# Two transformer layers on one core: 17 start-up weight loads move from SyncE's DMA queue to ScalarE's

## The chip, the cores and the metric

The kernel runs on one core of a Trainium2 chip. The metric is the device time of one execution in microseconds (us), lower is better. TensorE (PE), VectorE (DVE), ScalarE (ACT), GpSimd (POOL) and SyncE (SP) each run their own program in order and meet only through semaphores. Transfers between HBM and the on-chip memory are issued by an engine's program and carried out by 16 shared DMA engines; a semaphore rises when the data has landed.

## The reference

`x` is 64 sequences of 128 tokens with 256 features, `ctx` has the same shape. Two layers follow each other:

```
x = x + attn0(layernorm(x), ctx, ctx, mask)      # 16 heads of 16, biases on q, k, v, o
x = x + ffn0(layernorm(x))                       # 256 -> 1024 -> 256, weights quantised to -1, 0, 1
x = x + attn1(layernorm(x), ctx, ctx, lengths)   # no biases
x = ffn1(layernorm(x)) + x                       # chooses one of 8 experts by reconstruction loss
# quantisation in ffn0:
gamma = mean(abs(W)); Wq = clip(round(W / (gamma + eps)), -1, 1)
```

Quantising W1 and W2 (1 MB each) needs the whole matrix first, for gamma.

## The kernel before

The 64 sequences are worked through as 32 pairs. Everything that happens to one pair is cut into steps with a slot number from -14 to 77, and a new pair starts every 16 slots, so some five pairs are in flight. Each engine's program is a loop over the slots `t`; inside, `at(t, n)` picks the pair whose step `n` falls on slot `t`. The order in which an engine does its steps is thus written out by hand and fixed: a step that waits holds everything behind it on its engine.

SP issues every transfer, in one DMA queue. In program order at the start:

- `load(0)`: `xr`, `ctxT` and the two masks of pair 0 (L320 to L327).
- the seven loads of the list `EARLY` (L390): layer 0's `wk`, `wq`, `wv` and their biases. PE, DVE and ACT wait for all of them (semaphore `w_early`) before their loops.
- the two FFN matrices at L393 and L394, into `dif` (as `w1_ld`) and `hhl` (as `w2_ld`), tiles that later serve other ends; then the lengths (L395, L396) and `load(1)`.
- in the slot loop the round trips through HBM that bring queries and keys into another layout: `spill` (L334, `scr<-packed`) writes a pair's q or k out, `stack` (L354, `qs<-scr` or `ks<-scr`, four transfers) reads it back, and `maxima` (L370, `qs<-mrows`) puts row maxima under the queries.
- from slot -4 on, one transfer of the list `LATE` at the end of each slot (L432): 15 loads, among them `wo`, `wk`, `wq`, `wv` of layer 1, the base weights, the experts' `wd1s` and `wd2s`, and the biases `b1s`, `bd1s`, `bd2s`, which move element by element. Their first users wait for all 15 (`w_late`): PE at `output(0, 0)`, ACT, POOL and DVE later still.

DVE uses the FFN weights twice before the first scores: at slot -6 it waits for both matrices (`ffn_w_loaded`) and sums their absolute values (L1066, twice), turns the lengths into mask rows, and only then comes, in its program, to the query bias of pair 0 (`bias_q`, L817); POOL adds the sums over partitions (L579); at slot -2 DVE quantises (`quantise`, L769 to L778).

Pair 0's queries then go: DVE L817, ACT `high` (L613), DVE `low` (L832), SP `spill` (L334), SP `stack` (L354), and PE's scores (L1152), whose row maxima DVE takes (L859), with `exps` (L622) on ACT for the transposed scores (L1164).

```
if t == GAMMA_SLOT:
    dve.wait_ge(ffn_w_loaded, 32)
    for w, ld in enumerate((w1_ld, w2_ld)):
        nc.vector.tensor_reduce(gam[:, w:w + 1], ld, AX.X, ALU.add, ...)
```

Of the kernel before, what the change touches and what calls it, by code (L numbers as in the profile page):

```python
# [21 lines left out]
KD = D // P  # L22
# [3 lines left out]
KF = F // P  # L26
# [31 lines left out]
LATE_SLOT = -4  # L58
# [19 lines left out]
def ring(l, p):  # L78
    return (2 * p + 5 * l) % NR
# [16 lines left out]
def build(nc, x, lens, mask, mask_t, wq0, bq0, wk0, bk0, wv0, bv0, wo0, bo0, w1t, b1, w2t, b2,  # L96
          wq1, wk1, wv1, wo1, w_base, wd1, bd1, wd2, bd2, adapters, ctx_in, out):
    with ExitStack() as ctx:
# [6 lines left out]
        def sem(name):  # L105
            return ctx.enter_context(nc.semaphore(name))
# [84 lines left out]
        w1_ld = dif[:].rearrange("p e k t -> p (e k t)")  # L191
        w2_ld = hhl[:].rearrange("p a k t -> p (a k t)").bitcast(F32)
# [87 lines left out]
        w_early, w_late, ffn_w_loaded = sem("w_early"), sem("w_late"), sem("ffn_w_loaded")  # L280
# [12 lines left out]
        def rows(w):  # L293
            return w.rearrange("(k p) n -> p k n", p=P)
# [18 lines left out]
        @block.sync  # L313
        def _(sp):
            def load(p, ahead=False):
                if p < 2 and not ahead:
                    return
                if p >= NX:
                    sp.wait_ge(stored[p % 2], 16 * ((p - NX) // 2 + 1))
                sp.dma_start(xr[:, p % NX], xv[:, PB * p:PB * p + PB, :]).then_inc(x_loaded[p % 2], 16)  # L320
                k_ready[1].done(sp, p - NC)
                v_ready[1].done(sp, p - NC)
                sp.dma_start(ctxT[:, p % NC], ctx_in[p]).then_inc(ctx_loaded[p % 2], 16)
                mask_q.done(sp, p - 1)
                mask_k.done(sp, p - 1)
                sp.dma_start(mq_ld[:], mqv[:, PB * p:PB * p + PB, :]).then_inc(mask_loaded[p % 2], 16)
                sp.dma_start(mt_ld[:], mtv[:, PB * p:PB * p + PB, :]).then_inc(mask_loaded[p % 2], 16)  # L327

            def spill(l, j, p):
                ((k_high if j else q_high)[l]).done(sp, p)  # L330
                ((k_low if j else q_low)[l]).done(sp, p)
                if p >= 2:
                    sp.wait_ge(stacked[l][p % 2], STACK * (p // 2))
                sp.dma_start(scr[l][j][p % 2].rearrange("p m h d t -> (h d) p m t"), packed[l][j][:])\  # L334
                    .then_inc(scr_written[l][j], 16)

            def stack(l, j, p):
                dst = (ks if j else qs)[:, ring(l, p)]
                if l:
                    st_ready[0].done(sp, min(p + 1, NP - 1))  # L340
                    st_ready[1].done(sp, p - 3)
                else:
                    st_ready[1].done(sp, p - 4)
                    st_ready[0].done(sp, p - 3)
                sp.wait_ge(scr_written[l][j], 16 * (p + 1))
                if l and j and p == 0:
                    sp.wait_ge(len_steps, 4)
                    sp.dma_start(len_dram, len_rows[:]).then_inc(len_stored, 16)
                if j and p == 0:
                    sp.wait_ge(len_stored, 32 if l else 16)  # L350
                    sp.wait_ge(rows_set, 2)
                for n in range(4):
                    part = n % 2 if j else n // 2
                    sp.dma_start(dst[HD * n:HD * n + HD], scr[l][j][p % 2][part].rearrange("m h d t -> d (m h) t"))\  # L354
                        .then_inc(stacked[l][p % 2], 16)
                if j:
                    if l:
                        src = len_dram[PB * p:PB * p + PB].rearrange("(o b) t -> o (b t)", o=1)
                    else:
                        src = const_dram[0:1]  # L360
                    sp.dma_start(dst[MASK_ROW:MASK_ROW + 1], src.unsqueeze(1).to_broadcast([1, H, T]))\
                        .then_inc(stacked[l][p % 2], 16)

            def maxima(l, p, b):
                m_turned[l].done(sp, p, b)
                if l == 0 and p == 0 and b == 0:
                    sp.wait_ge(q_rows_set, 1)
                for n in range(4):
                    t0 = b * P + 32 * n
                    sp.dma_start(qs[MASK_ROW + 1:MASK_ROW + 3, ring(l, p), :, t0:t0 + 32],  # L370
                                 mrows[32 * n:32 * n + 32, l, b]).then_inc(m_landed[l][b], 16)

            def gather(p):
                up_ready.done(sp, p - 1)
                for b in range(PB):
                    expert_found.done(sp, p, b)
                    e = sp.value_load(lidx[0:1, b, 0:1], min_val=0, max_val=E - 1)
                    sp.dma_start(adapter[:, b], adapters[bass.ds(e, 1)].rearrange("a p n -> p (a n)"))\
                        .then_inc(gathered, 16)

            def store(p):
                y_ready.done(sp, p)
                if p >= 2:
                    sp.wait_ge(stored[p % 2], 16 * (p // 2))
                sp.dma_start(outv[:, PB * p:PB * p + PB, :], xr[:, p % NX]).then_inc(stored[p % 2], 16)

            load(0, True)
            with nc.allow_non_contiguous_dma(reason="biases, one or a few for each partition, once"):
                for dst, src in EARLY:
                    sp.dma_start(dst, src).then_inc(w_early, 16)  # L390
                sp.wait_ge(rows_set, 1)
                sp.dma_start(const_dram, const_rows[:]).then_inc(len_stored, 16)
                sp.dma_start(w1_ld.rearrange("p (k f) -> p k f", k=KD), rows(w1t)).then_inc(ffn_w_loaded, 16)  # L393
                sp.dma_start(w2_ld.rearrange("p (k d) -> p k d", k=KF), rows(w2t)).then_inc(ffn_w_loaded, 16)  # L394
                sp.dma_start(lens_c[:], lens.rearrange("(n a) -> n a", a=1)).then_inc(len_loaded, 16)  # L395
                sp.dma_start(lens_r[:], lens.rearrange("(a n) -> a n", a=1).to_broadcast([P, B])).then_inc(len_loaded, 16)  # L396
            load(1, True)
            for t in range(FIRST, END):
                for p in at(t, -14):
                    load(p)  # L400
                for p in at(t, 38):
                    spill(1, 0, p)
                for p in at(t, 6):
                    maxima(0, p, 0)
                for p in at(t, 38):
                    stack(1, 0, p)
                for p in at(t, 71):
                    gather(p)
                for p in at(t, -9):
                    spill(0, 1, p)  # L410
                for p in at(t, 7):
                    maxima(0, p, 1)
                for p in at(t, 24):
                    spill(1, 1, p)
                for p in at(t, -5):
                    stack(0, 1, p)
                for p in at(t, -4):
                    spill(0, 0, p)
                for p in at(t, 44):
                    maxima(1, p, 0)  # L420
                for p in at(t, -4):
                    stack(0, 0, p)
                for p in at(t, 76):
                    store(p)
                for p in at(t, 29):
                    stack(1, 1, p)
                for p in at(t, 45):
                    maxima(1, p, 1)
                if LATE_SLOT <= t < LATE_SLOT + len(LATE):
                    dst, src = LATE[t - LATE_SLOT]  # L430
                    with nc.allow_non_contiguous_dma(reason="biases, one or a few for each partition, once"):
                        sp.dma_start(dst, src).then_inc(w_late, 16)  # L432

            for k in range(2):
                sp.wait_ge(stored[k], 16 * (NP // 2))
# [147 lines left out]
        def _(act):  # L583
# [32 lines left out]
            def exps(l, p, j):  # L616
                st_ready[l].done(act, p, j)
                if l:
                    mix_ready[0].done(act, min(p + 2, NP - 1), j // 4)
                else:  # L620
                    mix_ready[1].done(act, p - 3, j // 4)
                nc.scalar.activation(pT[:, j], X[:], ACT.Exp, scale=SCALE).then_inc(exp_done[l].sem, 1)  # L622
# [51 lines left out]
                                         ACT.Relu, bias=adapter[R * b:R * b + R, b, AW - 1:AW]).then_inc(a_relu.sem, 1)  # L674

            act.wait_ge(w_early, 16 * len(EARLY))
            for t in range(FIRST, END):
                for p in at(t, 64):
                    squares(p, 0)
# [76 lines left out]
                    exps(1, p, 0)  # L756
                for p in at(t, 47):
                    exps(1, p, 1)

        @block.vector  # L760
        def _(dve):
# [682 lines left out]
```

## Time and profile before

| | |
|---|---|
| Runs | 1650.56, 1653.96, 1654.30 us; median 1653.96 |
| The profiled execution | 1655.75 us; its span, first to last instruction, 1654.0 us |
| TensorE busy | 1538.2 us, 93% of the span |
| VectorE, GpSimd, ScalarE busy | 1306.7, 1098.6, 892.6 us (79%, 66%, 54%) |
| DMA queues | one of transfers (SP's), 154.4 MB; two small ones for instructions |
| Mean granted TensorE clock | 0.965 |

Busy time is the sum of an engine's instruction times. The profile's page also shows the span in 40 slices of 41.35 us, a digit per slice in tenths. In the rows further down, "SPq" is a transfer being issued by SP (its duration is that of the issue, not of the data's way), "to landing" is the time from issue to the semaphore, and a name such as L1152 is a line of the kernel.

### The profile page before, as it was taken

How to read it: one execution, taken by the hardware profiler on the slowest of the kernel's cores; microseconds unless marked ns; L12 is line 12 of the kernel's file. 1: busy time of each engine (PE TensorE's matmuls, PEld its weight loads, DVE VectorE, ACT ScalarE, POOL GpSimd, SP SyncE). 2: the span in 40 equal slices, each digit the busy share in tenths (PEclk: the TensorE clock that was granted, in tenths of full speed). 3: DMA queues.
4: the chain of work that ended last, by engine and by line, in shares of the span. 5: the costliest groups of instructions: out<-in, count | busy, mean ns of one | idle time of the engine just before them, and what ended most of it. 6: DMA issues, size and time to landing. Idle time of an engine off the chain costs nothing.

```text
span 1654.0 us, 43794 instructions
## 1 busy us (share of the span) xinstructions
PE 1538.2 (93%) x15072; PEld 1270.5 (77%) x15072; DVE 1306.7 (79%) x5141; ACT 892.6 (54%) x2465; POOL 1098.6 (66%) x1197
## 2 busy tenths in 40 slices
PE   3588999999999999999999999999999999999865
PEld 2366888788888888888888888888888888887654
DVE  7456888888888888988888889888888898886552
ACT  0133555665555556655556566655565566555532
POOL 4476787766776777667767776667678766656300
PEclk7689999999999999999999999999999999999976
DMA  8447666456566665556566655565666555552320
GB/s 201 78 79 97 98 95 107 89 102 100 96 104 108 97 106 94 100 96 98 101 108 102 106 95 101 96 95 100 104 114 95 97 99 98 91 85 51 61 35 22
DMA packets 286479, 157.23 MB, mean 95 GB/s; under 512 B 39089, under 2 KB 281906, under 8 KB 286258
## 3 DMA queue, kind: packets, MB, share of 16 engines
q1 hardware_dynamic: 286258, 154.44, 55.3%
q8 instruction: 120, 1.97, 0.6%
q14 instruction: 101, 0.83, 0.2%
HBM read 111.36 MB, written 41.96 MB: 93 GB/s over the span
## 4 chain that ended last, share of the span: by engine, by line
PE 74%; DVE 9%; DMA 5%; issue 4%; POOL 3%; SPq 3%; ACT 1%; ACTq 0%; DVEq 0%; POOLq 0%
PE psD L1231 6%; PE psD L1189 6%; PE psD L1221 6%; PE psS L1152 6%; PE psV L1177 6%; PE psD L1210 6%; PE psD L1128 6%; PE psX L1164 6%; PE psD L1136 6%; PE psD L1202 5%; PE psD L1118 5%; DMA qs<-scr 4%; PE psD L1255 4%; PE psD L1101 3%; DVE dump L859 2%
## 5 line engine op out<-in xcount | busy, mean ns | idle before, releaser
L515 POOL TENSOR_TENSOR pT<-pT,keep 128x512 f32<-128x512 f32 x256 | 320.9, 1269 | 90.7 <-ACT pT L622 90.6
L622 ACT ACTIVATE pT<-psX 128x512 f32<-128x512 f32 x512 | 305.2, 596 | 110.7 <-PE psX L1164 105.3
L500 POOL TENSOR_SCALAR xn<-xr,mv,rstd 128x256 f32<-128x256 f32 x256 | 311.1, 1223 | 10.4
L474 POOL TENSOR_SCALAR veps<-mv 128x2 f32<-128x2 f32 x128 | 29.0, 226 | 360.1 <-DVE mv L794 357.8
L859 DVE CUSTOM_DVE_ANT_0 dump<-psS,bias 128x128 bf16<-128x128 f32 x1024 | 234.2, 283 | 23.3 <-PE psS L1152 21.7
L1152 PE MATMUL psS<-ks,qs 65*128 65x128 f16 x2048 | 202.0, 222 | 35.5 <-DMA qs<-scr 33.3
L925 DVE SCALAR_TENSOR_TENSOR dif<-psD,bd2s,xT 128x256 f32<-128x256 f32 x512 | 213.8, 466 | 13.0 <-PE psD L1231 12.9
L666 ACT ACTIVATE dif<-dif 128x256 f32<-128x256 f32 x512 | 207.6, 414 | 26.1 <-DVE dif L925 23.2
L1164 PE MATMUL psX<-qs,ks 67*128 67x128 f16 x2048 | 200.5, 220 | 14.2 <-ACT pT L622 10.1
L1152 PEld LDWEIGHTS psS<-ks,qs 65*128 65x128 f16 x2048 | 147.1, 99 | 85.3 <-issue 41.4
L851 DVE TENSOR_REDUCE mx<-psS 128x4 f32<-128x512 f32 x256 | 169.6, 671 | 23.2 <-PE psS L1152 23.0
L1164 PEld LDWEIGHTS psX<-qs,ks 67*128 67x128 f16 x2048 | 140.2, 98 | 49.1 <-ACT pT L622 17.3
L599 ACT ACTIVATE xT<-psD 128x512 f32<-128x512 f32 x96 | 57.2, 596 | 199.4 <-PE psD L1101 199.3
L520 POOL TENSOR_TENSOR hhl<-work,hhl 128x512 f16<-128x512 f32 x128 | 147.7, 1159 | 18.1 <-ACT hhl L652 15.4
L613 ACT ACTIVATE packed<-psD 128x512 f16<-128x512 f32 x96 | 57.3, 597 | 175.9 <-PE psD L1128 77.5
L1177 PE MATMUL psV<-pT,v 128*32 128x128 f32 x4096 | 139.9, 278 | 10.3 <-POOL pT L515 4.6
L1231 PE MATMUL psD<-hd,wd2s 64*128 64x256 f32 x1024 | 146.0, 404 | 2.6 <-DVE dif L925 2.6
L1118 PE MATMUL psD<-ctxT,wk 128*128 128x256 f32 x512 | 127.0, 392 | 11.2 <-DMA bvb<-in_bv 10.9
L1189 PE MATMUL psD<-wo,attT 128*128 128x256 f32 x512 | 130.4, 400 | 5.3 <-DVE attT L894 5.3
L1202 PE MATMUL psD<-xs,w1q 128*128 128x256 f16 x1024 | 132.9, 272 | 1.2 <-DVE xs L907 1.2
L646 ACT ACTIVATE work<-psD,b1s 128x256 f32<-128x256 f32 x256 | 107.8, 478 | 46.9 <-PE psD L1202 42.6
L1136 PE MATMUL psD<-wv,ctxT 128*128 128x256 f32 x512 | 131.3, 401 | 1.0 <-DVE packed L832 1.0
(96 smaller groups left out, 3125.8 us busy)
## 6 DMA issues: line engine op xcount, KB each, us to landing
scr<-packed SPq DMA_DIRECT2D x128, 256.0 KB, 2.9
ks<-scr SPq DMA_DIRECT2D x256, 128.0 KB, 5.4
qs<-scr SPq DMA_DIRECT2D x256, 128.0 KB, 4.3
adapter<-in_adapters SPq DMA_DIRECT2D x64, 192.5 KB, 2.5
xr<-in_x SPq DMA_DIRECT2D x32, 256.0 KB, 2.8
ctxT<-in_ctx SPq DMA_DIRECT2D x32, 256.0 KB, 2.7
qs<-mrows SPq DMA_DIRECT2D x512, 2.0 KB
out_y<-xr SPq DMA_DIRECT2D x32, 256.0 KB, 5.3
```

The source lines that it names most:

```text
L500: nc.gpsimd.tensor_scalar(xn[:, XN[s], b], xr[:, p % NX, b], mv[:, s, b, 0:1], rstd[:, s, b:b + 1], ALU.subtract, ALU.mult).then_inc(norme ...
L515: nc.gpsimd.tensor_tensor(blk, blk, keep[:, p % 2, j // 4].unsqueeze(1).to_broadcast([P, 4, P]), ALU.mult).then_inc(masked.sem, 1)
L622: nc.scalar.activation(pT[:, j], X[:], ACT.Exp, scale=SCALE).then_inc(exp_done[l].sem, 1)
L859: ins = nc.vector.tensor_tensor_reduce(out=dump[:, a], in0=S[:, a * P:a * P + P], in1=bias0[:, p % 2, b], scale=1.0, scalar=-3e38, op0=ALU ...
L925: nc.vector.scalar_tensor_tensor(out=dif[:, e % 4, k], in0=bank[f"rec{e}"][:, k * T:k * T + T], scalar=bd2s[:, e, k:k + 1], in1=xT3[:, p % ...
L1136: ins = nc.tensor.matmul(dst[:, b * D:b * D + D], ctxT[:, p % NC, k * T + b * P:k * T + b * P + P], wv[l][:, k], start=(k == 0), stop=(k = ...
L1152: ins = nc.tensor.matmul(S[:, a * P:a * P + P], qs[0:MASK_ROW + 1, r, h, t0:t0 + P], ks[0:MASK_ROW + 1, r, h, t0:t0 + P], start=True, stop ...
L1164: ins = nc.tensor.matmul(X[:, a * P:a * P + P], ks[0:ROWS, r, h, t0:t0 + P], qs[0:ROWS, r, h, t0:t0 + P], start=True, stop=True)
L1177: ins = nc.tensor.matmul(V[32 * a:32 * a + 32, n * P:n * P + P], v2[l][:, b, n // 2 * UH + 2 * a + n % 2], pT[:, 4 * b + n, a * P:a * P + ...
L1189: ins = nc.tensor.matmul(dst[:, b * D:b * D + D], attT[:, l, b, k], wo[l][:, k], start=(k == 0), stop=(k == KD - 1))
L1202: ins = nc.tensor.matmul(dst[:, m * T:m * T + T], w1q[:, k, f0:f0 + P], xs16[:, part, k], start=(n == 0), stop=(n == 2 * KD - 1))
L1231: ins = nc.tensor.matmul(dst[s][:, k * T:k * T + T], wd2s[half, m, k * P:k * P + P], hd[half, m], start=True, stop=True)
```

## The change

ACT issues the 17 transfers that SP issued before. The two FFN matrices come at the head of ACT's program, behind its wait for the early weights. The 15 late ones come at the end of the same slots, now of ACT's loop. They are in ACT's own DMA queue. Sizes, destinations, semaphores and waiters stay as they are.

```diff
@@ -390,8 +390,6 @@
                 sp.wait_ge(rows_set, 1)
                 sp.dma_start(const_dram, const_rows[:]).then_inc(len_stored, 16)
-                sp.dma_start(w1_ld.rearrange("p (k f) -> p k f", k=KD), rows(w1t)).then_inc(ffn_w_loaded, 16)
-                sp.dma_start(w2_ld.rearrange("p (k d) -> p k d", k=KF), rows(w2t)).then_inc(ffn_w_loaded, 16)
                 sp.dma_start(lens_c[:], lens.rearrange("(n a) -> n a", a=1)).then_inc(len_loaded, 16)
@@ -426,10 +424,6 @@
                 for p in at(t, 45):
                     maxima(1, p, 1)
-                if LATE_SLOT <= t < LATE_SLOT + len(LATE):
-                    dst, src = LATE[t - LATE_SLOT]
-                    with nc.allow_non_contiguous_dma(reason="biases, one or a few for each partition, once"):
-                        sp.dma_start(dst, src).then_inc(w_late, 16)
@@ -674,6 +668,8 @@
             act.wait_ge(w_early, 16 * len(EARLY))
+            nc.scalar.dma_start(w1_ld.rearrange("p (k f) -> p k f", k=KD), rows(w1t)).then_inc(ffn_w_loaded, 16)
+            nc.scalar.dma_start(w2_ld.rearrange("p (k d) -> p k d", k=KF), rows(w2t)).then_inc(ffn_w_loaded, 16)
             for t in range(FIRST, END):
@@ -756,6 +752,10 @@
                 for p in at(t, 47):
                     exps(1, p, 1)
+                if LATE_SLOT <= t < LATE_SLOT + len(LATE):
+                    dst, src = LATE[t - LATE_SLOT]
+                    with nc.allow_non_contiguous_dma(reason="biases, one or a few for each partition, once"):
+                        nc.scalar.dma_start(dst, src).then_inc(w_late, 16)
```

Two places show what this does to the programs. The first is the start of ACT's program. Before, ACT goes from the copy of the queries (L613) straight to the first exponentials (L622):

```order
L609 ACT_TABLE_LOAD
L609 ACTIVATE packed<-psD,bks 128x256 x2
L599 ACTIVATE xT<-psD 128x512
L613 ACTIVATE packed<-psD 128x512
L622 ACTIVATE pT<-psX 128x512
```

In the changed kernel (its lines are 6 lower in this part: L607 is the old L613, L616 the old L622):

```order
L671 DMA dif<-in_w1t 128x2x1024
L672 DMA hhl<-in_w2t 128x8x256
L603 ACT_TABLE_LOAD
L603 ACTIVATE packed<-psD,bks 128x256 x2
L593 ACTIVATE xT<-psD 128x512
L607 ACTIVATE packed<-psD 128x512
L758 DMA wo<-in_wo 128x2x256
L758 DMA b2b<-in_b 128x256
L758 DMA b1s<-in_b 128x8x1
```

The FFN matrices stand ahead of all of ACT's work, and behind the queries' copy come ten late loads (three are shown) before the first exponentials; the other five lie between the exponentials of pair 0.

The second place is SP's program between the maxima of pair 0 and the round trip of pair 1. Before:

```order
L370 DMA qs<-mrows 2x16x32 x4
L432 DMA wd1s<-in_wd 128x8x64
L334 DMA scr<-packed 128x4x256
L370 DMA qs<-mrows 2x16x32 x4
L432 DMA bd2s<-in_bd 128x8x1 x2
L432 DMA wd2s<-in_wd 64x4x256 x2
L354 DMA ks<-scr 16x16x256 x4
```

In the changed kernel:

```order
L370 DMA qs<-mrows 2x16x32 x4
L334 DMA scr<-packed 128x4x256
L370 DMA qs<-mrows 2x16x32 x4
L354 DMA ks<-scr 16x16x256 x4
L361 DMA ks<-const_dram 1x16x256
L334 DMA scr<-packed 128x4x256
L354 DMA qs<-scr 16x16x256 x4
```

Four late loads no longer stand ahead of `ks<-scr` of pair 1, nor, in the queue, ahead of its write and read of the queries.

## Rows read from the trace of the kernel before

**Rows 1.** The page: busy time, and the span in 40 slices

```profile
PE 1538.2 (93%) x15072; PEld 1270.5 (77%) x15072; DVE 1306.7 (79%) x5141; ACT 892.6 (54%) x2465; POOL 1098.6 (66%) x1197
...
PE   3588999999999999999999999999999999999865
```

**Rows 2.** Stretches: busy us (count) by engine, PE's clock, DMA share, GB/s

```profile
24.00:26.00 2.00, 0.00 (x0) 0.00 (x0) 1.16 (x4) 0.34 (x1) 0.78 (x2) 0.50 0.55 47
...
26.00:34.00 8.00, 0.00 (x0) 0.00 (x0) 7.65 (x8) 0.00 (x0) 1.23 (x1) 0.50 0.93 127
...
34.00:40.00 6.00, 3.88 (x23) 2.92 (x24) 4.63 (x37) 0.00 (x0) 2.09 (x4) 0.50 1.18 285
...
48.00:56.00 8.00, 4.38 (x22) 3.50 (x23) 1.12 (x5) 2.28 (x4) 5.75 (x6) 0.57 0.44 80
...
63.00:70.00 7.00, 1.38 (x28) 0.92 (x19) 1.91 (x5) 0.00 (x0) 0.00 (x0) 0.50 0.92 110
...
400.00:500.00 100.00, 99.70 (x990) 83.34 (x989) 86.16 (x351) 60.12 (x172) 73.62 (x82) 1.00 0.58 100
```

**Rows 3.** The chain that ended last, 0 to 80 us: start, us, what

```profile
17.83 4.38 DVE gam L1066 x2
...
22.84 0.88 DVE psD L817 x2
23.74 0.60 ACT packed L613
...
25.14 2.28 DMA scr<-packed
...
28.77 5.52 DMA qs<-scr
...
58.99 4.55 DMA scr<-packed
```

**Rows 4.** Transfers issued between 5 and 13 us: KB, us to landing

```profile
hhl<-in_w2t SPq DMA_DIRECT2D x1, 1024.0 KB, 9.9
...
mt_ld<-in_mask_t SPq DMA_DIRECT2D x1, 128.0 KB, 6.7
```

**Rows 5.** Timeline around the early loads: start, duration, engine, what

```profile
7.12 0.46 SPq L394 DMA_DIRECT2D hhl<-in_w2t  x1
...
10.92 3.06 PEld L1118 LDWEIGHTS psD<-ctxT,wk 128*128 128x128 f32 x8 [10.92 <-DMA bvb<-in_bv]
...
12.54 1.04 SPq L327 DMA_DIRECT2D mt_ld<-in_mask_t  x1
```

**Rows 6.** Timeline: the late loads on SP, and DVE's last quantising step

```profile
29.26 0.45 SPq L432 DMA_DIRECT2D wo<-in_wo  x1
...
32.67 1.23 DVE L778 TENSOR_SCALAR w2q<-hhl 128x2048 f16<-128x2048 f32 x1
```

**Rows 7.** Timeline of SP's queue between 48 and 57 us

```profile
48.73 0.37 SPq L334 DMA_DIRECT2D scr<-packed  x1
...
51.83 1.04 SPq L432 DMA_DIRECT2D bd2s<-in_bd  x2
52.91 1.40 SPq L432 DMA_DIRECT2D wd2s<-in_wd  x2
54.35 2.07 SPq L354 DMA_DIRECT2D ks<-scr  x4
```

**Rows 8.** Timeline of ACT from the queries' copy on

```profile
45.30 0.60 ACT L622 ACTIVATE pT<-psX 128x512 f32<-128x512 f32 x1 [20.96 <-PE psX L1164]
...
53.65 0.60 ACT L622 ACTIVATE pT<-psX 128x512 f32<-128x512 f32 x1 [2.92 <-PE psX L1164]
```

**Rows 9.** The chain again, 70 to 250 us: PE's steps at both clocks

```profile
71.50 3.53 PE psD L1189 x8
...
82.08 3.52 PE psD L1136 x8
...
225.47 1.73 PE psD L1189 x8
```

## The prediction

> **What bounds the kernel now.** I read the page first. TensorE is busy 93% of the span, and its slices stand at 9 except for the first four and the last few [rows 1]. The stretches say the same: from 400 to 500 us TensorE works 99.70 of 100 us at the full clock, and the DMA engines are busy 0.58 [rows 2]. All 17 moved transfers lie in the first 60 us, so the steady part is out of their reach. What they can do is move the moment at which the pipeline gets going, and since pair 0 is followed by every other pair in a fixed order, I take a shift there to reach the end whole. So the view that decides is the chain of waits over the first 80 us. The reader is to see in it that TensorE is not what is waited for: from 26 to 34 us it does nothing at all [rows 2], and the chain runs through DVE's sums of the FFN weights (17.83, for 4.38 us), the query bias (22.84), two copies, the write to HBM (25.14) and the read back that lands at 28.77 + 5.52 = 34.29 us [rows 3]. Transfers and the order on DVE bound this part.
>
> **The change part by part.**
>
> *FFN matrices issued later.* Before, the second is issued at 7.12 and lands 9.9 later, at 17.0 [rows 4, 5]. DVE comes to it at 17.83 [rows 3], so 0.8 us are to spare. Now ACT issues both only when the early weights are there, which is when TensorE starts, at 10.92 [rows 5]. Issue takes some 0.46 each, so the second leaves at about 11.4. If it still took 9.9 it would land at 21.3, 3.5 us after DVE asks. If it landed within the spare time, it would cost nothing; those are my ends, 0 and +3.5. I take the value by work: the DMA engines carried the same bytes in the old order, with pair 1's masks last, and these landed at 12.54 + 6.7 = 19.2 [rows 4, 5]. Now pair 1's loads go first, and the matrices last, with a small gap before them: 19.8. That is **+2.0** over 17.83. All of it is on the path, since the query bias stands behind the sums in DVE's program. The quantising behind it ends at 32.67 + 1.23 = 33.90 [rows 6] and moves by as much, and so stays hidden under the queries' trip.
>
> *SP's first loads earlier.* Without the two issues the lengths and pair 1's loads leave 0.9 us earlier. The lengths are read only behind the sums, pair 1's input much later: 0.
>
> *Ten late loads before the first scores.* Before, SP issues them from 29.26 on [rows 6], behind the four reads of the queries in the same queue. They carry 1.97 MB (six matrices of 256 x 256 floats, 256 KB of `wd1s`, a bias of 128 KB, two small ones), and flow mostly after the queries have landed: 127 GB/s up to 34 us, 285 from 34 to 40 [rows 2]. Now ACT issues them as soon as the queries' copy is done, at 24.34 before [rows 3] and 26.3 after the shift, while the write of the queries goes out only at 27.1 and their reads at 29.4. They are ahead in time and in another queue. If the queue of their own were served behind SP's, they would cost nothing. If they all went first, at 285 GB/s, they would cost 6.9 us. Those are the ends. Between them I add up the engines' work: from about 28 us on, 1 us for the write, some 4.5 for the reads, 6 for the late loads, 11.5 in all, so that the last is done at 39.6. Undisturbed the reads would land at 36.3. The queries need not be last; of the 3.3 I take **+3.0**, nearer to the whole since the late loads have the head start. The price is paid on the path: TensorE waits for exactly this landing [rows 3]. The Trainium skill bears on this term (DMA: Bandwidth & Descriptors, Queues, rings and completion order): each DMA engine takes turns between the rows of queues that have work, a packet at a time. By that rule the term is between 2 and 3.3 and the sum stays near mine; by the order that one queue shows in the rows, carried over to two, it would be 0 and the sum 3 lower. No row here shows two data queues at once.
>
> *Five late loads off SP's queue.* At 51.83 and 52.91 SP issues four loads, in 1.04 + 1.40 us, and only at 54.35 does it come to reading back pair 1's keys, which it wrote at 48.73 [rows 7]. The queries' write at 58.99 then takes 4.55, against 2.28 for the same write at 25.14 [rows 3], because the keys' reads are still under way before it. Without the four, those reads start 2.5 us earlier, into engines with room (a share of 0.44 from 48 to 56 us [rows 2]). The write gets back at most 4.55 - 2.28 = 2.3; nothing if ACT's copies of the same loads fill the gap. I take **-2.0**, since the first write shows what an undisturbed one needs. The read behind it, as long as pair 0's, I leave as it is.
>
> *Issue time on ACT.* 15 issues in the loop at some 0.45 each. Ten fall into a wait of 20.96 us for the first transposed scores [rows 8]; the others stand between exponentials, of which the fifth waits 2.92 us for TensorE, which itself waits for the maxima's transfer [rows 8]. Hidden: 0; uncovered, the five would cost 2.3. The last late load would land near 64 us; its first reader, TensorE's output projection, starts at 71.5 [rows 9]. The two FFN issues end before ACT's first input is there: 0.
>
> The sum is +2.0 + 3.0 - 2.0 = **+3.0 us** on the profiled execution's 1655.75, or 1658.8. That execution lies 1.8 above the median 1653.96, so I predict a median of **1657.0**. A measurement of this kernel tells about 0.3%, 5 us, from no change.
>
> The Trainium skill (same page, Issuing engines are not separate DMA queues) speaks against the change as a whole: transfers from several engines run on the same 16 DMA engines and interleave, and only the issue time of the sequencer is saved. By it, the gain is bounded by the 2.5 us of issue time above, and the FFN delay stays; the rows agree so far, as the DMA engines are busy 0.93 and more while the queries travel [rows 2].
>
> **The rivals.**
>
> *The late loads starve the queries' trip (slower).* Place: the write and reads of pair 0's queries. Price: the full 6.9 us, with the FFN delay at its upper end, 3.5, and the gain of 2.0: +8.4 on the median, 1662.4. It decides from the point at which contention and FFN delay together exceed 7 us, 5 more than the gain of 2.0. For it: from 26 to 34 us the engines are busy already at only 127 GB/s [rows 2], so the small pieces of the reads are dear, and every packet between them delays. Against it: the engines have pauses between write and read.
>
> *The second queue is free (no change).* ACT's queue is served in the pauses, contention is 0, the FFN delay 2.0 and the gain 2.0 cancel: 1654.0. Also the case in which the two queues behave like one. For it: the engines' share is only 0.55 from 24 to 26 us [rows 2], about the time at which they wait for the queries to be written. Against it: the late loads now leave before the queries' write.
>
> *The clock holds (faster).* From 63 to 70 us TensorE has little to do and the clock granted is half, 0.50 [rows 2]; the output projection then takes 3.53 us, where it takes 1.73 at the full clock, and the values, a step of as many matmuls, 3.52 [rows 9]. If the shorter round trip of pair 1 keeps the clock at 2.4 GHz instead of 1.2, 2 x 1.8 = 3.6 us come back; with the FFN matrices landing in time, no contention and the full 2.3: 0 + 0 - 2.3 - 3.6 = -5.9, 1648.1. For it: the idle time is just what shrinks. Against it: about 4 us of idleness would remain of some 6, and the clock stands low from the stretch's start.
>
> **How the numbers follow.** My forecast has 0.54, starving 0.22, the free queue 0.16, the held clock 0.08. The predicted time is the first one's, 1657.0. Slower by over 5 us (above 1658.9) takes the starving case and 0.04 of mine, whose sum could be 2 us more: 0.26. Faster (below 1649.0) is the clock's 0.08. The rest, 0.66, is no change. The range goes from 1649.5, just short of the fastest case, to 1664.0, which holds the starving case and nearly the sum of all upper ends (3.5 + 6.9 = +10.4, 1664.4).
>
> **What would show it.** In the changed kernel's profile: DVE's first sum starts near 19.8 and waits for the FFN load; the queries' reads of pair 0 land near 39 us instead of 34.3, with the late loads beside them; the write of pair 1's queries takes some 2.5 us instead of 4.55; the stretch from 400 to 500 us is as before. I am wrong if DVE's sum starts at 17.8 or past 21.3, if the first scores start before 37 or after 42 us, if the clock's low stretches change in number, or if the shift at 100 us is not that of the end.

## The result, and the profile after

The changed kernel takes 1657.11 us (median of 16 runs, 1655.22 to 1663.41). The kernel before, run between them on the same chip, takes 1649.92 (16 runs, 1646.80 to 1657.28). The ratio is **1.0043, 95% interval 1.0031 to 1.0055**: 7.2 us slower. The predicted 1657.0 is next to the measured median, but not for the predicted reason. I forecast +3.0 us on a kernel of 1654; it was +7.2 on a kernel of 1650. The 1653.96 came from three runs, and the profiled 1655.75 lies 5.8 above the median of 16. Two errors cancelled, and the sum has to be judged by its steps.

The page of the changed kernel, the answer to [rows 1], with the two data queues (packets, MB, share of the engines' time):

```profile
PE 1531.9 (93%) x15072; PEld 1266.9 (77%) x15072; DVE 1306.6 (79%) x5141; ACT 893.3 (54%) x2465; POOL 1102.1 (67%) x1197
...
PE   1577999999999999999999999999999999999865
...
q1 hardware_dynamic: 276898, 149.57, 53.4%
q10 hardware_dynamic: 9360, 4.87, 1.1%
```

The engines' work is what it was. Only the first slices of TensorE are thinner: 1577 where they were 3588. The stretches, with the columns of [rows 2]:

```profile
26.00:34.00 8.00, 0.00 (x0) 0.00 (x0) 7.06 (x13) 0.60 (x1) 0.76 (x2) 0.50 0.69 191
34.00:40.00 6.00, 0.00 (x0) 0.00 (x0) 2.94 (x3) 0.00 (x0) 3.71 (x2) 0.50 1.10 206
...
63.00:70.00 7.00, 4.77 (x52) 3.40 (x50) 3.38 (x8) 2.39 (x5) 3.41 (x3) 0.83 0.30 81
400.00:500.00 100.00, 99.63 (x1008) 82.96 (x998) 86.21 (x352) 58.49 (x163) 73.45 (x81) 1.00 0.55 95
```

From 34 to 40 us TensorE now does nothing, where it worked 3.88 us [rows 2]; from 400 to 500 us nothing has changed. The row from 63 to 70 us isn't the answer to its counterpart in [rows 2]: all work stands 6 to 7 us later, so it holds another piece of it (TensorE is busy 4.77 us in it, where it was 1.38). The chain of waits, as [rows 3]:

```profile
5.77 3.81 DMA bvb<-in_bv
9.60 0.45 ACTq L671
10.08 11.10 DMA hhl<-in_w2t
21.21 4.48 DVE gam L1066 x2
...
28.61 4.67 DMA scr<-packed
...
34.62 6.42 DMA qs<-scr
41.09 0.62 PE psS L1152 x4
...
57.58 4.17 DMA qs<-mrows
...
68.08 2.29 DMA scr<-packed
...
76.89 1.01 PE psS L1152 x8
77.90 3.53 PE psD L1189 x8
```

Read it against [rows 3] step by step. The sums start at 21.21 instead of 17.83 (+3.4). The write of pair 0's queries takes 4.67 instead of 2.28 (+2.4), their reads 6.42 instead of 5.52 (+0.9). The first scores start at 41.09. Before, they started at 34.33, so the shift is +6.8. The write of pair 1's queries fell from 4.55 to 2.29, as forecast, and yet pair 1's scores, at 76.89, are 6.4 later than the 70.50 of before: the distance between the two is nearly the same, 36.2 before and 35.8 after. The output projection behind them (L1189) takes 3.53 us, as before [rows 9].

One operation of GpSimd shows that the shift stays for at least 900 us. It is the same one of the same pair, in each kernel's timeline; first before, then after (lines are 6 lower after):

```profile
109.10 0.23 POOL L474 TENSOR_SCALAR veps<-mv 128x2 f32<-128x2 f32 x1 [0.68 <-DVE mv L794]
...
1006.04 0.23 POOL L474 TENSOR_SCALAR veps<-mv 128x2 f32<-128x2 f32 x1 [6.24 <-DVE mv L794]
```

```profile
115.28 0.23 POOL L468 TENSOR_SCALAR veps<-mv 128x2 f32<-128x2 f32 x1 [0.67 <-DVE mv L794]
...
1012.34 0.23 POOL L468 TENSOR_SCALAR veps<-mv 128x2 f32<-128x2 f32 x1 [6.23 <-DVE mv L794]
```

It is +6.2 at 109 us and +6.3 at 1006. After that this pair of executions draws together: the same operation of a later pair stands at 1542.95 before and 1547.31 after, +4.4, and the spans are 1654.0 and 1653.4, so that the changed kernel even ends 0.6 earlier. In the second pair of profiles (below) the two places are at +6.3 and +7.5, and the spans end 12.2 apart. Single executions thus drift by several us against each other, whatever the start. The largest piece of it here is the tail, where TensorE waits again and the clock granted to it differs. The last 94 us, before and after:

```profile
1560.00:1654.00 94.00, 60.14 (x430) 44.70 (x430) 37.95 (x109) 32.89 (x121) 6.75 (x8) 0.76 0.14 30
```

```profile
1560.00:1654.00 94.00, 59.62 (x455) 44.64 (x454) 41.06 (x118) 36.83 (x133) 7.96 (x9) 0.83 0.14 30
```

The granted clock is 0.76 in the one and 0.83 in the other, and the tail is some 5 us longer in the one of before. The medians count, not this pair of executions.

### The profile page after: what moved, and what is told of

It reads as the page before. It is cut to its first block, busy times and chain, and to the rows that moved or that the text cites. A ratio compares the mean times of both kernels' runs of the same rounds, so it can differ in the third digit from the quotient of the medians.

```text
span 1653.4 us, 43793 instructions
## 1 busy us (share of the span) xinstructions
PE 1531.9 (93%) x15072; PEld 1266.9 (77%) x15072; DVE 1306.6 (79%) x5141; ACT 893.3 (54%) x2465; POOL 1102.1 (67%) x1197
## 4 chain that ended last, share of the span: by engine, by line
PE 74%; DVE 8%; issue 6%; DMA 5%; POOL 3%; SPq 2%; ACT 1%; POOLq 0%; ACTq 0%; DVEq 0%
PE psD L1231 6%; PE psS L1152 6%; PE psD L1221 6%; PE psD L1189 6%; PE psV L1177 6%; PE psD L1210 6%; PE psD L1128 6%; PE psX L1164 6%; PE psD L1136 6%; PE psD L1202 5%; PE psD L1118 5%; PE psD L1255 4%; PE psD L1101 3%; DMA qs<-scr 3%; DVE dump L859 2%
## 5 line engine op out<-in xcount | busy, mean ns | idle before, releaser
L616 ACT ACTIVATE pT<-psX 128x512 f32<-128x512 f32 x512 | 305.2, 596 | 115.0 <-PE psX L1164 109.6
L925 DVE SCALAR_TENSOR_TENSOR dif<-psD,bd2s,xT 128x256 f32<-128x256 f32 x512 | 213.6, 465 | 12.3 <-PE psD L1231 12.2
L1164 PEld LDWEIGHTS psX<-qs,ks 67*128 67x128 f16 x2048 | 140.3, 97 | 52.5 <-issue 18.3
L607 ACT ACTIVATE packed<-psD 128x512 f16<-128x512 f32 x96 | 57.4, 598 | 178.7 <-PE psD L1128 75.9
L1189 PE MATMUL psD<-wo,attT 128*128 128x256 f32 x512 | 130.8, 401 | 5.0 <-DVE attT L894 4.9
```

Of the source, the lines that this page charges most:

```text
L925: nc.vector.scalar_tensor_tensor(out=dif[:, e % 4, k], in0=bank[f"rec{e}"][:, k * T:k * T + T], scalar=bd2s[:, e, k:k + 1], in1=xT3[:, p % ...
L1164: ins = nc.tensor.matmul(X[:, a * P:a * P + P], ks[0:ROWS, r, h, t0:t0 + P], qs[0:ROWS, r, h, t0:t0 + P], start=True, stop=True)
L1189: ins = nc.tensor.matmul(dst[:, b * D:b * D + D], attT[:, l, b, k], wo[l][:, k], start=(k == 0), stop=(k == KD - 1))
```

## The experiments

Twelve runs were made in three groups, ten of other kernels and one more of each of the two. The interval of each ratio belongs to the runs of before of its own group (medians 1652.38, 1653.10 and 1651.72). "Distance" is the time from pair 0's first scores to pair 1's.

**The FFN loads alone, and the late loads alone.** The first kernel makes only the edit at L393, the second only that at L432.

> Only the two FFN matrices are issued by ScalarE, behind its wait for the early weights; the 15 late loads stay on SyncE. Theory: two separate prices, the FFN matrices' lateness and the late loads' company for the queries' trip. Then this one shows the first alone: DVE's sums start near 21.2 us instead of 17.8, the write of pair 0's queries takes 2.3 us as before, the first scores start near 37.8 (34.3 + 3.4), and the time is about 3.5 us over the kernel before (ratio 1.002). Rival: having a second queue in use at all, or the late loads alone, makes the loss: then the first is 7 us over and the second 0.

> Only the 15 late loads are issued by ScalarE; the FFN matrices stay on SyncE as before. Theory: sums at 17.8 as before; the write of pair 0's queries takes 4.5 us or so instead of 2.3, the reads 6.4 instead of 5.5, first scores near 37.6 (34.3 + 3.3); the second transfer of the maxima takes 4 instead of 1.7 us; pair 1's write of the queries 2.3 instead of 4.6. In all about +3 us (ratio 1.002). Rival, a free second queue: first scores at 34.3, time 2 to 3 us under before.

Measured: 1655.25 us, ratio 1.0022 (1.0009 to 1.0035), and 1656.47 us, 1.0032 (1.0019 to 1.0045). The chain of the kernel with the FFN loads alone:

```profile
10.02 11.22 DMA hhl<-in_w2t
...
28.67 2.29 DMA scr<-packed
...
32.30 5.20 DMA qs<-scr
37.55 0.62 PE psS L1152 x4
```

And of the kernel with the late loads alone:

```profile
25.64 3.72 DMA scr<-packed
...
30.80 8.64 DMA qs<-scr
39.49 0.62 PE psS L1152 x4
...
56.28 3.86 DMA qs<-mrows
...
66.73 2.29 DMA scr<-packed
```

The first shifts the first scores by 3.2 us and leaves the queries' trip alone (2.29 and 5.20). The second shifts them by 5.2, nearly all in that trip: 3.72 and 8.64 against 2.28 and 5.52 [rows 3], to 39.49, where 37.6 was expected. Both parts cost. The second costs less inside the whole change (+3.3) than alone (+4.6 in the trip). What differs in the traces is a third party, the reads of pair 0's keys. Alone, the first late load leaves at 24.25 us, while these reads, issued from 20.69 on and landing 4.3 us after their issue, are still under way, and the engines' share is 1.12 from 26 to 28 us. Inside the whole change it leaves at 27.22, and from 26 to 28 us the share is 0.05. That this is the reason was not tried by itself.

**The late loads held back.** ACT waits for the reads of pair 0's queries before its first late load, once with the whole change and once with the late loads alone.

```diff
+                if t == LATE_SLOT:
+                    act.wait_ge(stacked[0][0], STACK)
                 if LATE_SLOT <= t < LATE_SLOT + len(LATE):
```

> The full change, but ScalarE waits, before its first late load, until pair 0's queries and keys have been read back. Theory: the late loads' company is the second price, so it goes: first scores at 34.3 + 3.4 = 37.7 and not 41.1, write of pair 0's queries in 2.3 us; the time 3 us under the full change, 3 to 4 over before. If the second queue slows transfers by being there, the write stays near 4.6 us.

> The FFN matrices stay on SyncE, the late loads are issued by ScalarE, but only once pair 0's queries have been read back. So SyncE's queue is relieved at no price before the first scores. Theory: first scores at 34.3; pair 1's write of the queries takes 2.3 instead of 3.8 to 4.6 us, but the gain is given back at the second transfer of the maxima, which lands some 20.5 us behind the first scores instead of 18.6 to 19.9; pair 1's scores 36.2 us behind the first, as in all runs so far (35.2 to 36.8); ratio 1.000 within 0.0015. Rival: the late loads on ScalarE cost on their own, as the run with the wait and the late FFN matrices (1.0040 with first scores only 2.8 late) may say; then 1.002 or more.

Measured: 1656.76, 1.0040 (1.0027 to 1.0053), and 1653.58, 1.0005 (0.9993 to 1.0018). The chain of the first of the two:

```profile
28.77 2.29 DMA scr<-packed
...
32.41 4.70 DMA qs<-scr
...
55.43 2.17 DMA qs<-mrows
```

The write is back at 2.29 and the reads at 4.70, below the 5.52 of before. The first scores start at 37.16, 3.9 us earlier than in the changed kernel. So the company of the late loads is the cause of the trip's length: with the order in time as the only difference, it goes. With the late loads alone held back, and the FFN matrices at their old place, the first scores start at 33.79, and the late loads on ACT cost nothing that the interval shows, but bring nothing either. The time of the first kernel doesn't fit its profile: its first scores are 2.9 us late, at which other kernels lose some 4 us, and its ratio, from only 5 runs, stands for 6.6. That remains open.

**SP's queue relieved without a second queue.** SP issues two late loads a slot, so that they are done before pair 1's round trip.

```diff
-                if LATE_SLOT <= t < LATE_SLOT + len(LATE):
-                    dst, src = LATE[t - LATE_SLOT]
+                if t >= LATE_SLOT:
+                    for dst, src in LATE[2 * (t - LATE_SLOT):2 * (t - LATE_SLOT) + 2]:
```

> Nothing moves to ScalarE: the kernel before, with two late loads a slot on SyncE, so that all 15 are issued before the first transfer of the maxima and none stands ahead of pair 1's round trip. Theory: the gain of the change (pair 1's write of the queries in 2.3 instead of 4.6 us, its read half a us shorter) is SyncE's order and needs no second queue: first scores at 34.3, the scores of pair 1 near 67.8 instead of 70.5, if the five loads do not delay the first maxima (ready at 40.96; the queue may be busy until then or 2 us longer). Time 1 to 3 us under before (ratio 0.998 to 0.9995). Rival: the gain comes only with a queue of its own; then no change.

Measured: 1652.87, 1.0003 (0.9986 to 1.0019). Its chain:

```profile
53.01 1.70 DMA qs<-mrows
...
61.27 2.29 DMA scr<-packed
```

The write of pair 1's queries takes 2.29 here as well, and it wins nothing: it starts at 61.27, 2.3 later than at 58.99 [rows 3], and ends at 63.56, where before it ended at 63.54. The distance is 36.4, against 36.2. The expectation of a gain of 1 to 3 us failed. Part of the later start has a reason of this kernel's own: the first transfers of the maxima leave at 43.43, behind the last late loads, where they left at 40.96 before. But the short write that I had booked as a gain comes with a later start here too.

**The two kernels again**, unchanged, in a group of their own.

> The kernel before, once more, as a control and for a second profile of it. Theory: the start is the same from run to run (first scores at 34.3 within 0.3 us), but the clock granted in thin stretches (50 to 86 us, and the last 94 us) is not, and moves single runs by some 4 us; so the ratio is 1.000 within 0.0015, and the span of the profile differs from 1654.0 by up to 5 us without any step of the first 45 us having moved. Rival: the profiled execution of before was typical, and the median differs for another reason: then the spans agree within 1 us.

> The full change, once more, beside the others on one chip and for a second profile. First scores at 41.1 within 0.3, second transfer of the maxima in 4.2, pair 1's write of the queries in 2.3 us; ratio 1.003 to 1.0055. If the second transfer of the maxima comes out near 2 us here, its 4.2 was chance and is struck from the account.

Measured: 1652.28, 0.9996 (0.9978 to 1.0014), and 1660.24, 1.0052 (1.0034 to 1.0070). The result holds, and the first shows what such a comparison can tell: the same kernel against itself, known to about 0.2%. In the changed kernel's second chain:

```profile
10.14 11.44 DMA hhl<-in_w2t
...
29.00 4.27 DMA scr<-packed
...
34.62 7.26 DMA qs<-scr
...
60.65 1.94 DMA qs<-mrows
```

The write and the reads are long again (4.27, 7.26), and the first scores come at 41.92. The transfer of the maxima takes 1.94, where it took 4.17 in the first execution. It is issued 3.1 us later instead, and the landings, at 61.75 and 62.59, are 20.7 us after the first scores in both. By the test set above, the 4.2 is struck as a fixed cost; the 20.7 is what repeats.

**The FFN loads first of all on ACT**, ahead of its wait for the early weights:

```diff
-            act.wait_ge(w_early, 16 * len(EARLY))
             nc.scalar.dma_start(w1_ld.rearrange("p (k f) -> p k f", k=KD), rows(w1t)).then_inc(ffn_w_loaded, 16)
             nc.scalar.dma_start(w2_ld.rearrange("p (k d) -> p k d", k=KF), rows(w2t)).then_inc(ffn_w_loaded, 16)
+            act.wait_ge(w_early, 16 * len(EARLY))
```

> The full change, with the two FFN matrices issued before ScalarE's wait for the early weights, that is, first of all. Theory: the wait makes them late (issued at 9.6, the DMA engines only 0.45 busy from 8 to 12 us), not the queue. Now they run beside the early weights: 3.9 MB in one go at some 350 GB/s is there by 13 to 14 us, the early weights land 1 to 3 us later than 9.6, and DVE's sums, no longer waiting for a load, start at 18 to 19.5; first scores near 39 instead of 41.1; time 2 us under the full change (ratio 1.003). Rival: a queue of ScalarE delivers slowly whatever is asked of it; then the matrices still land near 20.

Measured: 1661.87, 1.0061 (1.0039 to 1.0083). Its chain:

```profile
7.61 7.00 DMA bvb<-in_bv
...
21.56 4.38 DVE gam L1066 x2
...
34.66 8.66 DMA qs<-scr
```

The second matrix, issued at 1.29, lands 10.9 later at 12.2, 9 us earlier than in the changed kernel, and the sums start no earlier, at 21.56: now the early weights wait, until 7.61 + 7.00 = 14.61 instead of 9.58. From 4 to 12 us the engines move 363 GB/s, so this is not idleness but a matter of who goes first. What DVE does before its sums needs those weights. So ACT's queue isn't slow by itself (the rival falls), but the 2 us that the theory promised did not come either.

**The small late loads first.** The same 15, the small and element-by-element ones among the first six.

```diff
+        LATE = [LATE[i] for i in (0, 1, 2, 8, 11, 12, 3, 4, 5, 6, 7, 9, 10, 13, 14)]
```

> The full change with the late loads in another order: the three biases that move element by element (b1s, bd1s, bd2s) are among the ten before the first scores, and base weights and experts' matrices among the last five. Theory: the two bd2s loads of 1024 pieces each, issued beside the second transfer of the maxima, stretch it from 1.7 to 4.2 us; without them it takes about 2 to 3 (the matrices in their place still share the engines), and the scores of pair 1 come 1 to 2 us sooner than 76.9; against that the small pieces now share the engines with pair 0's queries, first scores at 41 to 42.5. Time: within 1.5 us of the full change. Rival: bytes count, not pieces: then the second transfer takes 4 or more, since 0.8 MB more stand beside it.

Measured: 1665.11, 1.0077 (1.0059 to 1.0096), the slowest of all. Its chain:

```profile
29.02 3.63 DMA scr<-packed
...
33.99 9.41 DMA qs<-scr
```

The write is shorter than in the changed kernel, the reads take 9.41 against 6.42 and 7.26. The order of the late loads alone adds 2 to 3 us to the reads and brings the first scores to 43.45, later than expected, with the element-wise pieces now among those issued beside them. The ten loads ahead of the first scores carry 0.5 MB less than in the changed kernel (`wb` and half of `wd1s` have gone behind), so it is not their bytes. The time was expected within 1.5 us of the full change and is 4.9 above it.

**A plain delay.** The kernel before, in which DVE takes the two sums a second time, into a tile that nothing reads. Its computation is otherwise the whole one.

```diff
+                    for w, ld in enumerate((w1_ld, w2_ld)):
+                        nc.vector.tensor_reduce(spare[:, w:w + 1], ld, AX.X, ALU.add, apply_absolute_value=True)
```

> The kernel before with two more sums over the FFN weights on VectorE, into a spare tile that nobody reads: a pure delay of 4.6 us ahead of the query bias, with no transfer moved. Theory: a shift of the first scores reaches the end whole; first scores at 38.7 to 38.9, ratio 1.0027 (1.0012 to 1.0042). Rival: the steady part takes up a shift, and what costs in the changed kernel is something else; then the ratio is 1.000.

Measured: 1655.61, 1.0027 (1.0009 to 1.0045). Its chain:

```profile
22.11 4.39 DVE spare L1070 x2
...
33.06 5.15 DMA qs<-scr
38.26 0.62 PE psS L1155 x4
```

Without any transfer being moved, first scores 3.9 us later cost 0.27%, 4.5 us (1.5 to 7.4). What is lost before the first scores is lost at the end: the shift as a whole fits, a loss of nothing doesn't, and the interval is too wide to tell the rate more closely.

**Shorter work ahead of the query bias.** The opposite: one of the two sums goes to the next slot, behind the query bias, and half of the quantising to slot 9.

```diff
                 if t == GAMMA_SLOT:
...
+                if t == GAMMA_SLOT + 1:
+                    nc.vector.tensor_reduce(gam[:, 1:2], w2_ld, AX.X, ALU.add, apply_absolute_value=True)\
+                        .then_inc(gamma_part, 1)
```

> The kernel before with VectorE's order changed: the query bias of pair 0 comes after the first sum instead of after both and the mask rows, and W2 is quantised in VectorE's idle time behind the maxima of pair 0 (slot 9) and not before the first scores. Theory: the bias waits for TensorE's queries only (20.6), so the trip of the queries starts 2.2 us sooner; first scores at 32.1, time 2 us under before (ratio 0.9987). Rival: the 4.2 us of quantising at slot 9 delay pair 1's query bias and give it back; then pair 1's scores are no earlier than 36.2 us plus 34.3, and the ratio is 1.000.

Measured: 1652.85, 0.9999 (0.9984 to 1.0014). The bias doesn't come earlier, for what it waits for in the timeline, first on DVE, then on PE:

```profile
22.81 0.88 DVE L817 SCALAR_TENSOR_TENSOR psD<-anyb,bqs,psD 128x256 f32<-128x256 bf16 x2 [1.86 <-PE psD L1133]
...
18.99 3.78 PE L1133 MATMUL psD<-xT,wq 128*128 128x256 f32 x8 [0.69 <-ACT xT L599]
```

TensorE's queries end at 22.77, and the bias starts at 22.81, as before at 22.84 [rows 3]. The edit isn't what moved them. In this execution the early weights let TensorE start at 11.84 instead of 10.92 [rows 5], and the matmuls take 3.78 us, where they took 2.98 (from 17.61 on) in the first profile of before and 3.78 (from 18.05 on) in its second. So the 20.6 of the expectation was one execution's; the second has the queries at 21.83. TensorE's queries are ready only 1 to 2 us ahead of the bias, and so the sums alone don't set this point. Pair 1's scores come 37.2 us after pair 0's, the longest distance of all, which fits the rival; how much of it the moved quantising makes was not tried.

**The FFN loads late, but in SP's queue**, behind `load(1)`:

```diff
             load(1, True)
+            sp.dma_start(w1_ld.rearrange("p (k f) -> p k f", k=KD), rows(w1t)).then_inc(ffn_w_loaded, 16)
+            sp.dma_start(w2_ld.rearrange("p (k d) -> p k d", k=KF), rows(w2t)).then_inc(ffn_w_loaded, 16)
```

> Everything on SyncE, the FFN matrices issued last of the early transfers, behind pair 1's loads: late, but in the one queue. Theory: what costs is the place in time, not the queue: issued at about 10, they land at 19 to 20 (less than the 21.2 of ScalarE's queue if the DMA engines have fewer gaps), sums at 19 to 20, first scores at 35.6 to 36.8, ratio 1.001 to 1.002. Rival: the one queue delivers them as early as before (17 to 17.8); then only ScalarE's queue is at fault, and the ratio is 1.000.

Measured: 1657.69, 1.0026 (1.0011 to 1.0040). The engines from 8 to 12 us, in the kernels before, after, and this one:

```profile
8.00:12.00 4.00, 1.08 (x3) 0.90 (x4) 2.96 (x6) 0.00 (x0) 1.00 (x2) 1.00 0.97 261
```

```profile
8.00:12.00 4.00, 2.38 (x6) 1.93 (x7) 3.19 (x6) 1.28 (x1) 1.92 (x4) 1.00 0.45 130
```

```profile
8.00:12.00 4.00, 2.61 (x6) 2.17 (x7) 3.18 (x6) 0.00 (x0) 1.92 (x4) 1.00 0.56 170
```

The last two columns are the DMA engines' share and the GB/s. This kernel, with one queue, issues its second matrix at 10.53 and has it at 20.13; the sums start at 20.16, +2.3 of the +3.4 of after. It is mostly the time of issue that costs, not the second queue, which can have at most the other 1.1. The times agree: 1.0026 here, and 1.0022 with the same two loads on ACT. Nor is it ACT's wait as such: nothing waits for the early weights here, the matrices stand behind the issues of pair 1's loads, and the engines' share is 0.56 all the same. Bulk loads that aren't issued yet leave them half empty, whatever holds the issue.

**All of them together.** Over the twelve runs and the changed kernel, the time lost against before grows with the shift of the first scores from 34.26 us (the mean of the two profiles of before): some 1.1 us for each us of shift and 0.5 us besides, correlation 0.95, 11 of the 13 within 1.3 us of the line. The two outside are the held-back late loads (+2.8) and the small ones first (+1.9). No kernel beats the one before; its equals are the two late loads a slot, the late loads held back alone, and the split sums.

## Why the prediction was right or wrong

- **What bounds the kernel: right.** The start sets the shift, and in the medians it reaches the end. Two landmarks (+6.2, +6.3), the plain delay (3.9 us of shift, 4.5 at the end, interval 1.5 to 7.4) and the line through 13 comparisons show it; single executions drift too much to show it at their ends.
- **FFN matrices issued later: mechanism right, size wrong.** +2.0 was booked, +3.4 measured (the ends were 0 and +3.5). The step that failed is "with a small gap before them". The early weights did land earlier, at 9.58 instead of 10.87, and ACT issued at 9.60 and 10.08; but then the engines, at 130 GB/s instead of 261 over 4 us, had about 0.5 MB to catch up, and the second load took 11.1, not 9.9 [rows 4]. I had counted the bytes ahead of the matrices and not the idleness. They landed at 21.2, close to my upper bound of 21.3, which was simply the 9.9 of before from the later issue.
- **Ten late loads: right.** +3.0 was booked, +3.3 measured (+3.7 in the second profile), between 0 and 6.9, and holding the loads back removes it. The size has some luck in it: moved alone, the same loads lengthened the trip by 4.6, beside the reads of the keys, which the sum of the engines' work had left out. It fell on the write (+2.4) more than on the reads (+0.9), where I had expected the reads alone. The Trainium skill's rule on turns between queue rows (DMA: Bandwidth & Descriptors, Queues, rings and completion order), by which the term was 2 to 3.3, agrees with the trace as far as that goes: in the changed kernel the queries' write (issued at 28.61) and `wk` (at 28.63), 256 KB each and in different queues, landed 4.7 and 4.4 us after their issue, so two queues with work share the engines and neither waits for the other. That turns are taken packet by packet no row here shows.
- **Five late loads off SP's queue: wrong.** -2.0 was booked. The write is 2.3 us shorter, exactly as forecast, and nothing was gained: the distance is 35.2 to 37.2 us in all 14 profiles, and its mean is 36.3 both in the six that have late loads of SP ahead of pair 1's trip and in the eight that have none. The step that failed is the last one, that the time saved on the write is saved on the path. For that the trip must not begin later, and it does: counted from the first scores, the write starts after 25.6 us and takes 3.9 in the six (means), and starts after 27.3 and takes 2.3 in the eight, so that it ends at the same moment. What it follows, by 6.1 to 6.6 us in every profile, is the landing of the second maxima: 18.4 to 20.2 us after the first scores in the six, 20.4 to 21.4 in the eight. Some of this differs between executions and isn't the change's (the last section has one piece of 1 us). In three of the eight (the changed kernel, the late loads alone, those held back alone) the maxima leave as early as in the first profile of before, 16.5 to 16.9 us after the first scores, and take 3.7 to 4.2 us instead of 1.71; in the others they leave 18.3 to 18.8 after and take 1.7 to 3.1. That the remaining late loads beside the maxima hold the landing back is likely for the three; with two late loads a slot none is left beside them, the transfer takes 1.70, and its late landing has the reason given there. It was not tried by itself and stays open.
- **Issue time on ACT and SP's first loads: 0, right as far as the profile shows.** The Trainium skill (same page, Issuing engines are not separate DMA queues) had said that only issue time could be saved, and no gain at all is to be seen.
- **The sum.** With the measured terms it is 3.4 + 3.3 + 0 = +6.7; measured is +7.2, and the line's 1.1 us for each us of shift would account for the rest. That the time came out at 1657.1, next to 1657.0, is luck: a baseline 4 us too high met a shift 4.2 us too small. My forecast mechanism held with one term too small and one that doesn't exist. The outcome, slower by over 0.3%, is near the price of my rival of starvation (+8.4), to which, with a little of mine, I gave 0.26; no change had 0.66.
- **The rivals.** The free second queue falls: the write took 4.67. Starvation at its full price falls as well: 3.3 of 6.9. The held clock did not happen where its price was: the output projection takes 3.53 us at 77.90 and the values 3.52 at 88.49, as before [rows 9]. The 0.83 from 63 to 70 us, against 0.50, belongs to other work, in which TensorE was busier. In the second profile the projection takes 3.27, a gain of 0.3 of the 1.8 booked for it.
- **What was to show it.** The first sum at 21.21 is between the forecast 19.8 and the bound of 21.3 (the second profile, at 21.60, is past it); the reads landed at 41.04, not near 39; pair 1's write took 2.29, forecast 2.5; the shift at 109 us is that at 1006 us, but not that of the end, in either pair of profiles. By my own test, then, the account was not wholly right, and the test itself was poor: single executions of one kernel end up to ten us apart, and fixed stretches of the clock hold other work once everything has shifted.

## What to carry to other kernels

A bulk load that is issued late leaves the DMA engines half empty in the meantime (a share of 0.45 and 0.56 instead of 0.97), and its first reader pays (+3.4 us here). Issued ahead of everything it is no better, since the loads that are needed sooner then land later (the early weights at 14.61 instead of 10.87). Of the three places tried for the two matrices, that of the kernel before was the best: in the one queue, directly behind the loads that are needed sooner. A second issuing engine brought no time in any of these kernels, but it took away the order that one queue gave for free: background loads then travel beside a short trip that everybody waits for, until something holds them back. And before booking a shorter transfer as a gain, ask whether it starts at the same time; measure the distance between two points of the chain instead.

## What the runs showed of the hardware that was not expected

- The clock granted in thin stretches varies between executions of one kernel: 0.75 and 0.79 from 1560 to 1650 us in the two profiles of before. Single runs of before lie between 1646.8 and 1657.3 us in the main comparison alone, ten us apart, more than the whole effect of 7.2; how much of that the clock makes was not measured. Three runs were too few to name the baseline to 4 us.
- A write of 256 KB, 2.28 us long, nearly doubles beside bulk loads of another queue (4.67, 4.27), and reads of 4.70 us without company take 6.42 to 9.41 with it, most when element-wise pieces are in it.
- One small operation of DVE, an update of the maxima (L868), decides 1 us on the path to the second maxima. It takes 0.17 to 0.23 us in seven profiles and 1.15 to 1.25 in the other seven. What separates them is in the traces: it is long in every profile in which GpSimd's three multiplications `pT<-pT,keep` (L515 in the kernel before) have started ahead of it, by 0.05 to 0.15 us, and then it ends 1.3 us after their start; it is short in every profile in which they start after it. The kernel before shows both, in its first profile and in its second:

```profile
48.77 0.18 DVE L868 SCALAR_TENSOR_TENSOR m<-mx,m 128x16 f16<-128x16 f32 x1
...
48.95 3.71 POOL L515 TENSOR_TENSOR pT<-pT,keep 128x512 f32<-128x512 f32 x3
```

```profile
48.89 3.71 POOL L515 TENSOR_TENSOR pT<-pT,keep 128x512 f32<-128x512 f32 x3
...
49.02 1.16 DVE L868 SCALAR_TENSOR_TENSOR m<-mx,m 128x16 f16<-128x16 f32 x1
```

In the second, a third of the 3.71 us from 48.89 on is over at 50.13, when the first multiplication is done, and L868 ends at 50.18. So which of two engines comes first by 0.1 us costs or saves 1 us, in unchanged kernels too. No run moved the one operation on purpose, so the cause is read from 14 traces and not tried.
